# Routing one block sooner, the first block in another order, and four sends in flight: a gated attention block with a mixture of experts on one core

## What is computed

```python
def attn(x):                       # x is xn; a second norm inside
    uv = silu((norm(x) * ln_w + ln_b) @ uv_w.T + uv_b)    # 640 columns
    u, v, base = split(uv, 256, 256, 128)
    q, k = rope(base * gamma[i] + beta[i])               # i = 0, 1
    kernel = square(relu(q @ k.T / sqrt(S) + w[rel]))    # 512 x 512 per block
    return (u * (kernel @ v)) @ o_w.T + o_b + x
def ffn(x):
    probs = sigmoid(x @ W_router)                        # 8 experts, top 2
    out = sq_relu(x @ W_sh_up) @ W_sh_down               # shared expert
    for e in range(8):
        out += combine[:, e:e+1] * (sq_relu(x @ W_up[e]) @ W_down[e])
    return out
out = x + attn(xn) + ffn(xn)
```

## Time and profile before

| what | us |
|---|---|
| median of 3 runs | 433.27 (432.76 to 434.15) |
| the profiled execution | 432.69 |
| its span | 430.5 |
| TensorE matmuls busy | 369.2 (86%) |
| VectorE busy | 238.2 (55%) |
| ScalarE busy | 227.2 (53%) |
| POOL busy | 151.2 (35%) |
| mean granted TensorE clock | 0.954 |

### The profile page before, as it was taken

How to read it: one execution, slowest core, us unless ns; L and a number is a source line. 1 busy time by engine, 2 the same in 40 slices (tenths; PEclk the granted TensorE clock), 3 DMA queues, 4 the chain that set the end, 5 groups by cost and what they waited for, 6 DMA issues and landing times.

```text
span 430.5 us, 7290 instructions
## 1 busy us (share of the span) xinstructions
PE 369.2 (86%) x1970; PEld 280.1 (65%) x1971; DVE 238.2 (55%) x622; ACT 227.2 (53%) x421; POOL 151.2 (35%) x150
## 2 busy tenths in 40 slices
PE   1557899999899879989950499999999999999992
PEld 1345468676465636646520399999999999999840
DVE  3668877377988858758440133333333333333677
ACT  0354373675466635576520176666666666666520
POOL 3005220000000776764677024444444444444300
PEclk9989899999999998999995599999999999999997
DMA  6929800000000122146111112121212221211397
GB/s 142 266 71 273 177 0 2 1 0 2 0 0 2 45 68 94 46 131 203 45 50 50 50 46 70 56 68 56 68 56 68 56 68 50 74 56 43 108 293 210
DMA packets 50310, 34.00 MB, mean 79 GB/s; under 512 B 5876, under 2 KB 46708, under 8 KB 50293
## 3 DMA queue, kind: packets, MB, share of 16 engines
q1 hardware_dynamic: 43538, 23.71, 21.9%
q0 software_dynamic: 4352, 8.99, 6.3%
q10 hardware_dynamic: 2402, 1.10, 1.1%
HBM read 17.83 MB, written 15.95 MB: 78 GB/s over the span
## 4 chain that ended last, share of the span: by engine, by line
PE 44%; issue 23%; DMA 13%; POOL 8%; DVE 3%; ACT 0%; DVEq 0%; ACTq 0%; SPq 0%
PE bank L1269 15%; DMA slots_in<-work,slot_i 12%; POOL slots_in L982 8%; PE bank L1250 8%; PE bank L1004 5%; PE bank L1005 5%; PE bank L1006 5%; PE bank L1105 3%; PE bank L1243 2%; PE bank L1091 1%; DVE x_all L810 1%; DVE x_all L808 1%; PE bank L1068 1%; DMA slot_x<-slots_in 1%; PE bank L1040 0%
## 5 line engine op out<-in xcount | busy, mean ns | idle before, releaser
L982 POOL DMA_INDIRECT slots_in<-work,slot_i x64 | 68.0, 1062 | 113.8 <-issue 93.3
L991 POOL DMA_INDIRECT results<-work,dest x72 | 69.3, 963 | 95.8 <-DVE work L919 93.0
L1269 PEld LDWEIGHTS bank<-wdn,work 128*128 128x128 f32 x576 | 75.1, 191 | 6.0
L1269 PE MATMUL bank<-wdn,work 128*128 x576 | 75.7, 274 | 0.0
L919 DVE TENSOR_SCALAR work<-bank,row_sum 128x128 f32<-128x128 f32 x72 | 25.2, 350 | 84.0 <-PE bank L1269 82.1
L1105 PE MATMUL bank<-kern,v 128*128 128x512 f32 x128 | 60.3, 606 | 0.0
L592 ACT ACTIVATE work<-bank 128x512 f32<-128x512 f32 x72 | 43.3, 601 | 16.2 <-PE bank L1250 16.0
L598 ACT ACTIVATE work<-bank 128x512 f32<-128x512 f32 x72 | 43.1, 598 | 8.5 <-PE bank L1006 3.1
L586 ACT CAST sx_hi<-bank 128x128 fp32r<-128x128 f32 x72 | 19.0, 266 | 48.5 <-PE bank L1243 48.1
L1250 PE MATMUL bank<-cst,work 128*128 128x128 f32 x288 | 43.9, 275 | 0.0
L1105 PEld LDWEIGHTS bank<-kern,v 128*128 128x128 f32 x128 | 23.5, 197 | 22.0 <-issue 22.0
(11 more groups left out here) (162 smaller groups left out, 657.7 us busy)
## 6 DMA issues: line engine op xcount, KB each, us to landing
slots_in<-zeros SPq DMA_DIRECT2D x1, 4752.0 KB, 22.5
slot_x<-slots_in SPq DMA_DIRECT2D x36, 132.0 KB
work<-in_L_ffn_W_up SPq DMA_DIRECT2D x8, 256.0 KB, 3.1
wdn<-in_L_ffn_W_down SPq DMA_DIRECT2D x4, 512.0 KB, 7.4
wup_hi<-results SPq DMA_DIRECT2D x8, 256.0 KB, 5.1
wup_lo<-results SPq DMA_DIRECT2D x8, 256.0 KB, 5.2
out<-x_all SPq DMA_DIRECT2D x8, 256.0 KB, 3.1
results<-work,dest POOLq DMA_INDIRECT x72
```

What stands on the lines that cost most here:

```text
L982: pool.indirect_dma_start(slots_in, bass.IndirectOffsetOnAxis(slot_i[:, k, t:t + 1], 0), xs1[:, t, at], None, element_offset=k * 2).then_i ...
L991: pool.indirect_dma_start(results, bass.IndirectOffsetOnAxis(dest[:, at:at + 1], 0), slot_y[:, k, :], None).then_inc(returned[k], 16)
L1269: last = pe.matmul(P_Y[h][:, 0:D], hid_t[:, h, rows], wdn[:, of, c, :].rearrange("p a d -> p (a d)"), start=(c == 0), stop=(c == HC - 1))
```

## The change

It has four parts.

1. Ahead of turn 0 the first norm and the first rows come before the weights' bias on VectorE, and x1 before x2 on TensorE and ScalarE. The gates of block 0 come before its values. ScalarE's issues of the columns of uv_b go to SP. `score_bias` and its copies are gone: POOL spreads the bias on 128 partitions, all are written, and the load takes each row one element on.
2. Groups 1 to 7 of the first norm go from VectorE to ScalarE (`norm`), with a shift, mean times root, made by POOL. The roots are split in two.
3. Every step of the routing comes sooner: logits 2 and 3 in turn 0, choices and weights in turn 1, counts and slots in turn 2, owners in turn 3. The expert weights are split two to a turn in turns 3 to 6. `rotate_sum` of the next block is moved to the end of the turn before.
4. The sends take turns on four semaphores: each waits for the send four before it.

```diff
-    by_distance = nc.dram_tensor("by_distance", (1, 2 * T), F32).ap()
+    by_distance = nc.dram_tensor("by_distance", (P, 2 * T), F32).ap()
...
+        IN_FLIGHT = 2 * TOPK
+        tokens_sent = [sem(f"tokens_sent{k}") for k in range(IN_FLIGHT)]
...
+            if b == 0:
+                RING += gates + up + values
+            elif b == 1:
+                RING += values + [rt[5], up[0], rt[6], up[1]] + gates + [rt[7]]
...
+            if b == 0:
+                RING += [rt[1], ("x2", 1), rt[2], ("base", 1), ("bsw", 1), rt[3], ("x1", 1), rt[4]]
...
+            sp.dma_start(w_sb[:, :], w.rearrange("(a n) -> a n", a=1).broadcast_to([P, WREL])).then_inc(ld["w"], 16)
...
+            load_rows(1, FIRST, 12)
+            cols(uvb_c[:, 0:2], uv_b[0:EU].rearrange("(a p) -> p a", p=P))
...
+            sp.dma_start(cos_sin[:, :, :], consts[:, C_COS:C_W].rearrange("p (a t) -> p a t", a=2)).then_inc(ld["cos_sin"], 16)
             sp.dma_start(vb_bc[:, :], uv_b[EU:2 * EU].rearrange("(a e) -> a e", a=1).broadcast_to([P, EU])).then_inc(ld["wide"], 16)
+            load_rows(2, 12, 20)
             sp.wait_ge(ld["dist"], 16)
...
+            shifted = bass.AP(by_distance.tensor, by_distance.offset + P - 1, [[2 * T - 1, P], [1, BIAS_W]])
+            sp.dma_start(bias_t[:, :], shifted).then_inc(ld["bias"], 16)
...
-            for k in range(TOPK):
-                sp.wait_ge(tokens_sent[k], 16 * NT)
+            for lane in range(IN_FLIGHT):
+                sp.wait_ge(tokens_sent[lane], 16 * TOPK * NT // IN_FLIGHT)
...
+            def norm(g):
+                act.wait_ge(shift_made, {1: 1, 2: 2, 3: 2, 4: 2}.get(g, 3))
+                for t in range(g * TB, g * TB + TB):
+                    last = act.activation(xs1[:, t, X0:X0 + D], x_all[:, t, :], ACT.Identity, bias=shift[:, t:t + 1], scale=inv1[:, t:t + 1])
+                last.then_inc(xs1_act, 1)
...
+                if route == 1:
+                    routing_copied(5)
+                shared_relu(b, 0)
+                if route == 1:
+                    routing_copied(6)
+                shared_relu(b, 1)
+                v_silu(b)
+                if not first:
                     u_silu(b)
+                if route == 1:
+                    routing_copied(7)
...
                 if route == 1:
-                    routing_copied(5)
-                if 4 <= route < LAST:
-                    weights_hi(3 * route - 11)
-                    weights_hi(3 * route - 10)
-                    if route < LAST - 1:
-                        weights_hi(3 * route - 9)
+                    routing_probs()
+                if 3 <= route < LAST:
+                    weights_hi(2 * route - 5)
+                    weights_hi(2 * route - 4)
                 shared_relu(b, 2)
                 shared_relu(b, 3)
...
+                if route == 0:
+                    norm(1)
+                    norm(2)
+                    routing_copied(1)
                 if not last:
                     second_rows_hi(b + 1)
-                if route == 0:
-                    routing_copied(1)
                 shared_square(b, 2)
                 shared_square(b, 3)
-                if route == 1:
-                    routing_copied(6)
+                if route == 0:
+                    norm(3)
+                    norm(4)
+                    routing_copied(2)
                 if not last:
                     base_silu(b + 1)
+                    if route == 0:
+                        routing_copied(3)
                     first_rows_hi(b + 1)
                 if route == 0:
-                    routing_copied(2)
-                    routing_copied(3)
-                if route == 1:
-                    routing_copied(7)
-                    routing_probs()
+                    routing_copied(4)
+                    norm(5)
+                    norm(6)
+                    norm(7)
...
             turned_weights()
+            first_rows_hi(0)
             second_rows_hi(0)
+            weights_hi(0)
             value_weights()
-            output_weights()
             act.wait_ge(uvb_made, 1)
             act.wait_ge(ld["turn_cols"], 6 * 16)
             base_silu(0)
-            first_rows_hi(0)
-            weights_hi(0)
-            score_bias_kept()
             routing_copied(0)
+            u_silu(0)
+            output_weights()
             act.wait_ge(ld["ob"], 16)
             sequence_turns(act, turn)
...
+                link(var_made, dve.tensor_scalar(var_eps[:, tiles], var, EPS, None, ALU.add))
+                link(stat_chain, dve.reciprocal(per_var[:, tiles], var_eps[:, tiles]))
...
+                v_bias(b)
...
-                if route == 1:
-                    first_norm(5)
+                    statistics(2, 12, 20)
+                    dve.wait_ge(ld["bias"], 16)
...
                 if route == 0:
-                    first_norm(1)
-                if not last:
+                    variances(slice(FIRST, 20))
+                elif not last:
                     second_norm(b + 1)
                 kernel_square(b, 2)
                 kernel_square(b, 3)
                 if route == 0:
-                    first_norm(2)
-                    first_norm(3)
+                    second_norm(1)
                     statistics(3, 20, NT)
                 if route == 1:
-                    first_norm(6)
-                    first_norm(7)
+                    routing_first()
                 if route == 2:
-                    routing_first()
+                    routing_counts()
                 if route == 3:
-                    routing_counts()
-                if route == 4:
                     routing_owners()
...
+                if 3 <= route < LAST:
+                    weights_lo(2 * route - 5)
...
                 if route == 0:
                     variances(slice(20, NT))
-                    first_norm(4)
+                if route == 1:
+                    routing_second()
                 if route == 2:
-                    routing_second()
-                if route == 3:
                     routing_tiles()
                     routing_slots()
...
+                if 3 <= route < LAST:
+                    weights_lo(2 * route - 4)
                 if not last:
                     rotate_base(b + 1)
                     first_rows_lo(b + 1)
-                if route == 2:
+                    rotate_sum(b + 1)
+                if route == 1:
                     routing_weights()
...
+            first_norm(0)
+            second_norm(0, True)
+            dve.wait_ge(uv_copied, 1)
...
+            def root(to, of, tiles):
+                pool.tensor_tensor(to[:, tiles], of[:, tiles], minus_half[:, tiles], ALU.pow).then_inc(inv_made, 1)
+
+            def mean_shift(tiles, done):
+                pool.wait_ge(inv_made, done)
+                pool.tensor_tensor(shift[:, tiles], neg_mean[:, tiles], inv1[:, tiles], ALU.mult).then_inc(shift_made, 1)
...
-                    if t > 0:
-                        pool.wait_ge(tokens_sent[k], 16 * t)
+                    lane, turns = (t * TOPK + k) % IN_FLIGHT, (t * TOPK + k) // IN_FLIGHT
+                    if turns > 0:
+                        pool.wait_ge(tokens_sent[lane], 16 * turns)
...
+                if first:
+                    gates()
+                    first_up()
                 v_part(b, 0)
...
-                    uv_part("u0", b, 0)
-                    uv_part("u1", b, P)
+                    output_weights()
+                    pe.wait_ge(ld["wr"], 16)
...
+                if route == 1:
+                    routing_logits(4)
+                    routing_turned(5)
...
+                    gates()
                 if route == 1:
-                    routing_logits(2)
-                    routing_logits(3)
-                    routing_turned(4)
-                if route == 3:
+                    routing_logits(5)
+                    routing_turned(7)
+                    routing_logits(6)
+                if route == 2:
                     routing_counted()
...
                 if route == 1:
-                    routing_turned(5)
+                    routing_logits(7)
...
+                if first:
+                    pe.wait_ge(ow_made, 1)
                 values(b, 0)
+                if route == 0:
+                    routing_turned(1)
+                    values(b, 1)
                 if not last:
                     second_rows_turned(b + 1)
                 if route == 0:
                     routing_logits(1)
-                if route == 1:
-                    routing_turned(6)
-                values(b, 1)
+                    routing_turned(2)
+                    values(b, 2)
+                else:
+                    values(b, 1)
...
-                    routing_turned(7)
+                    routing_turned(3)
...
-                    routing_logits(6)
+                    routing_logits(2)
+                    routing_turned(4)
...
+                if route == 0:
```

(23 more changed lines are left out.)

196 lines of the change are left out of this document (78 added, 118 removed).

## The result

| | before | changed |
|---|---|---|
| median, us | 433.62 (4 runs, 432.76 to 434.15) | 401.78 (4 runs, 400.07 to 404.79) |
| the profiled execution | 432.69 | 402.41 |
| its span | 430.5 | 400.6 |
| PE matmuls busy | 369.2 (86%) | 366.8 (92%) |

The ratio is 0.9275, with a 95% interval from 0.9215 to 0.9335.

What follows compares the result with a forecast made beforehand. Sends bounded expert entry, 18.8 us behind attention. First block 7.5 and turns 9.8 sooner put entry at 206.4, 35.4 sooner; 1.0 of clock made 36.4 off 432.69: 396.3, plus 0.6 to the median, 397.0 us; range 391 to 405.

Steps and rivals of the forecast that it cites:

- What bounds it, and the sends: Before the experts: sends end last by 18.8 us; after the change, slot_x is there at 200, 5.7 ahead of attention.
- the first rival: Before the experts: sends still end last because POOL's issue is slow, four in flight gaining nothing; 401 us, chance 0.16.
- The first block: Block 0, up to turn 1: reordered norms and waits let turn 1 begin at 52.3, 7.5 us sooner (3.0 to 8.8).
- the bound of 2: Start of kernel: heavier load of w and write of by_distance delay all later landings by zero to about 2 us.
- Turn 1: Attention turn 1: 29.6 us from 30.33, with 2.0 of matmuls leaving, 0.9 added for routing weights, 0.4 for Silu's table.
- The upper end that I gave: Attention turn 1: at most 33.5 us, with all 5.2 us of select and weights in the open.
- Turn 2: Attention turn 2: 25.1 us, from 23.08 plus 0.7 of matmuls and 1.3 that the slots' chain holds the rotation.
- Turns 3 to 5: Attention turns 3 to 5: two expert weights each in place of three, waits gone, 23.3 us each, 69.9 in all.
- Turn 6: Last attention turn before the experts: moving rotate_sum earlier is worth 0, since TensorE is full.
- The hand-over: Entry into the experts: reading expert registers takes 0.7 us in the open after the last add, between 0 and 2.
- The clock: Expert loop: with no hole before it, TensorE's lower clock costs less, 1.0 us taken back, between 0 and 3.
- the turns keep their length: Attention turns: another wait takes the weights' place, so the 9.8 us gain is lost; 407 us, chance 0.04.

Runs made afterwards that it cites:

- the products: Fifteen matmuls whose results nobody reads, placed around the hand-over where TensorE would stand, added to mended: 396.51 us, ratio 0.9172.
- mended: Changed kernel with routing weights moved out of turn 1's end and block 7's rotation sum put behind block 6's gate: 398.81 us, ratio 0.9226.

## Why the prediction was right, and where it was off

The sum said 396.3 for the profiled execution, and that took 402.41. By its own steps:

- **What bounds it, and the sends.** Right. First send at 107.81 (108.1 forecast), the train 89.1 (87), the last at 196.88 (195), the load issued at 199.24, and TensorE enters on the last add. Each of the two edits was needed: without the sooner routing the sends end last by 12.5 us, with two in flight by 1.3. Four in flight was worth nothing in my sum, as what keeps the first rival away; taken away, it cost 4.0 in the median, of which the trace puts 1.3 down to the sends.
- **The first block.** 8.5 us sooner at turn 1 (51.28 against 59.76), 7.5 forecast. The places were right within 1.0: x2_lo 13.36 (12.4), base_silu 16.40 (15.6), sum 22.00 (22.3), qk_lo 25.16 (25), gate 51.35 (51). The rows of x landed at 6.23 in place of 4.46, behind the load of w and within the bound of 2. By the times in the changed kernel that alone cost x2_lo nearly nothing, since ScalarE came free of its table load only then. From qk_lo to the gate it was 26.2, forecast 26. My steps gave 8.2 at the gate and I took 7.5, nearer the low end; the gate came 7.8 sooner, and TensorE began turn 1 0.07 ahead of it, where before it stood 0.58 behind.
- **Turn 1.** 27.88, 29.6 forecast. TensorE was full. The choices hid; the weights' 0.9 and the table load's 0.4 belong to turn 2, and cost more there. The upper end that I gave, 5.2 us for choices and weights, is a wrong sum: the three terms (2.3, 3.1, 1.8) make 7.2.
- **Turn 2.** 28.78 against 25.1, the term most mis-sized: 3.7 of the 6.1 missing. The step that failed is the slack. I gave `routing_weights` 0.9 us of it ahead of `v_bias`; that is what `v_bias` waited for TensorE in turn 2 of the kernel before (0.91), which followed a turn 1 of 30.33 us, and the change shortens that turn. In turns 4 to 6 of the changed kernel `v_bias` begins 2.6 us into the turn, and TensorE takes the bank just then: there is none. At 4.03 (turn 3) TensorE stood 1.29, at 5.79 (turn 2) 3.14. The weights cost 1.95 where I charged 0.9, and the table load, for which I charged 0.4, accounts for the other 1.2. Then the clock fell, 1.39 for which I had no term. Against the forecast it is 0.5 more of matmuls, 3.14 of idle time for the 1.3 that I had put here for the slots, and the 1.39. Moving the weights away gave 3.34 back.
- **Turns 3 to 5.** 25.06, 23.67, 23.67 against 23.3 each: 2.5 over. The waits for expert weights are gone, as forecast. Turn 3 keeps a wait of 1.29 for `v_bias`, behind turn 2's counts and slots; I had put that 1.3 in turn 2. In the other two, the 0.37 is mostly matmuls: the same 91 count as 23.59 busy, and as 23.32 in turn 5 before, where I had only taken out the idle 1.25.
- **Turn 6.** +1.15 where I said 0: the moved sum stands ahead of the last gate on VectorE (sum at 204.31, gate at 205.44). I argued that TensorE is full; in the last turn it is not, since nothing follows but this block's own chain.
- **The hand-over.** 1.08 in the open, 0.7 taken.
- **The clock.** I took 1.0 us back, and got 0.5 worse. The hole went, but the small stalls of 1.60, 0.78 and 1.81 us that remained were enough for the lower level: 0.61 from 210.34 to 216.00. What it costs there is 0.9 to 2.4 us, by the distance from the last add to the second expert layer without the products (7.7 to 9.2) and with them (6.8).

Together −1.0 +4.5 +1.15 +0.4 +1.5, and 0.4 less around the span: 6.1, the whole difference. So the mechanism was right: the sends, the first block and the turns each moved the way the sum had them. Part of the nearness is luck: the first block gave 1.0 more than was taken, and hides as much of what the turns missed. Not tested apart are the norms on ScalarE and the expert weights split two to a turn.

Of the rivals, the one that the turns keep their length (407) came nearest to what went wrong: of 9.8 us forecast in turns 1 to 5, 5.3 came (129.06 against 134.39). The table load as priced by the Trainium skill (ScalarE: Activation LUTs, What ACT_TABLE_LOAD costs), 1.38 us of drain on top of 1.28, isn't in the row: 1.28 at 73.51, base_silu at 74.81, and 0.86 idle ahead, as ahead of turn 5 without a load (0.85). The 1.28 are seen in the start of base_silu, 1.26 later than in turn 5.

## What to carry to other kernels

When work is moved to the head or the tail of a stage, look for the one instruction behind it on that engine's queue that frees a buffer for the busiest engine, and read its slack from a stage as long as it will be after the change: here 0.9 us were read behind a turn of 30.33 us, and none were left behind one of 27.88. Slack is spent once, by all that comes late for that instruction: the weights on VectorE and the table load on ScalarE added up. Price a stall of TensorE with the matmuls behind it at the lower clock: here stalls of 3.14 us cost 1.4 us more in slow matmuls in the first profile, and turn 2 took 28.8 to 30.2 us over the five profiles that have this stall. And state the cover of a hidden transfer as a number: with half the semaphores the same sends ended last again.

## What the runs showed of the hardware

- Scattered sends of 128 rows, each issue 1.0 to 1.1 us: with two in flight POOL stood 20.5 to 27.2 us of some 100 for landings, with four 1.2 to 2.5.
- In the kernel before TensorE kept its 2.4 GHz level behind one stall of 2.14 us (turn 3, granted 1.00). It fell to 1.2 GHz behind one of 3.14 us, and at the hand-over behind three of 1.60, 0.78 and 1.81 us, one close behind the other (in mended 0.47, 0.78 and 1.81); with products in these it stayed at 2.4 GHz.
- A broadcast load of 64 KB, issued ahead of the first rows of x (0.73 and 1.19 us), went with a landing at 6.23, where with a load of 0.5 KB in its place it was 4.46; issued behind them it let them land at 3.69.
- A table load of 1.28 us on ScalarE showed nothing beside its own length: the next activation began 0.02 us behind it (73.51 + 1.28, 74.81).
